# Four normalised columns in the value projection, offsets beside their values, and constants and weights of the second half made inside the first

## The reference, cut

```python
# x: (2, 128, 128, 128); _gn: GroupNorm over 32 groups of 4 channels, no weights
x = x + _L0_conv_ref(_gn(x), qkv_w, qkv_b, proj_w, proj_b, bias_table)
x = x + _L1_conv_ref(_gn(x), value_proj_w, value_proj_b, offset_mask_w, offset_mask_b,
                     output_proj_w, output_proj_b)

# _L0: 16 x 16 windows, 8 heads
attn = softmax(einsum('whnd,whmd->whnm', q, k) * scale + bias[None])
out = einsum('whnm,whmd->whnd', attn, v) @ proj_w.T + proj_b

# _L1: deformable convolution, G = 8 groups, K = 9 taps
v  = xt @ value_proj_w.T + value_proj_b            # values of each pixel
om = xt @ offset_mask_w.T + offset_mask_b          # 8 x 9 x (dx, dy, mask) of each pixel
loc_x = px + kx + off[..., 0]; loc_y = py + ky + off[..., 1]
# four corners of each (loc_x, loc_y), weighted bilinearly, times the mask, summed over the taps
out = einsum('nhwkgc,nhwkg->nhwgc', sampled, mask_t).reshape(N, L, C) @ output_proj_w.T + output_proj_b
```

## Time and profile before

| what | value |
|---|---|
| median of three runs | 3287.48 us (3285.68 to 3289.9) |
| the profiled execution | 3290.47 us |
| its span, first to last instruction | 3288.8 us |
| PE busy | 2733.5 us (83%), 22424 matmuls |
| PEld busy | 2192.2 us (67%) |
| DVE busy | 2719.8 us (83%) |
| ACT busy | 1828.7 us (56%) |
| POOL busy | 1162.0 us (35%) |

### The profile page before, as it was taken

The page is one execution under the profiler, slowest core; times in us unless marked ns, Lnnn a source line. Parts: engine busy times, 40 slices in busy tenths (PEclk is TensorE's granted clock), DMA queues, the critical chain, the costliest instruction groups (busy, mean ns, idle before and its releaser), DMA issues.

```text
span 3288.8 us, 77998 instructions
## 1 busy us (share of the span) xinstructions
PE 2733.5 (83%) x22424; PEld 2192.2 (67%) x22424; DVE 2719.8 (83%) x6553; ACT 1828.7 (56%) x3486; POOL 1162.0 (35%) x1557
## 2 busy tenths in 40 slices
PE   1888889999999999995677989998946799999986
PEld 0555555565565556564566888887835688888885
DVE  3888888888888888885667999999945799999996
ACT  0888888888888888884143443333202443334420
POOL 3333233333333333332446231346232441115550
PEclk9999999999999999998988999999978899999998
DMA  7889897888888898895553233333374433333334
GB/s 182 158 157 163 166 148 138 139 140 143 138 141 142 141 139 143 140 144 116 183 158 91 89 99 101 99 103 84 89 261 134 144 101 101 97 101 95 102 89 160
DMA packets 351779, 432.59 MB, mean 132 GB/s; under 512 B 42352, under 2 KB 275200, under 8 KB 346480
## 3 DMA queue, kind: packets, MB, share of 16 engines
q1 hardware_dynamic: 339696, 423.85, 58.5%
q0 software_dynamic: 11904, 6.44, 1.5%
HBM read 283.33 MB, written 147.09 MB: 131 GB/s over the span
## 4 chain that ended last, share of the span: by engine, by line
DVE 24%; issue 10%; DMA 6%; PE 5%; POOL 3%; DVEq 1%; ACT 1%; POOLq 1%; SPq 1%; ACTq 0%
DVE prod L1635 17%; DMA vring<-vals 3%; DVE tt L1619 2%; PE sum_ps L1429 2%; DVE my L1614 2%; DMA vring<-attended 1%; DVE x L1646 1%; PE sum_ps L1384 1%; ACT d_xn L1518 1%; DMA o_sel<-off_out,pos 1%; PE om_ps L1347 1%; POOL gath L1209 1%; PE sum_ps L1333 1%; POOLq L1216 1%; DMA out<-x 0%
## 5 line engine op out<-in xcount | busy, mean ns | idle before, releaser
L623 ACT ACTIVATE prob<-sbias,nmax 128x256 f32<-128x256 f32 x2048 | 903.9, 501 | 203.4 <-DVE nmax L716 201.0
L716 DVE CUSTOM_DVE_ANT_0 sbias<-s_ps,nbias 128x256 f32<-128x256 f32 x2048 | 768.0, 420 | 212.8 <-PE s_ps L508 201.4
L1635 DVE TENSOR_TENSOR prod<-vring,wt_ps 128x1920 f32<-128x1920 f32 (+3 forms) x512 | 898.8, 1815 | 18.8 <-DMA vring<-vals 11.9
L1384 PE MATMUL sum_ps<-d_ident,prod 128*128 128x128 f32 x6400 | 773.0, 279 | 83.5 <-DVE prod L1635 83.4
L1384 PEld LDWEIGHTS sum_ps<-d_ident,prod 128*128 128x128 f32 x6400 | 732.0, 144 | 131.8 <-DVE prod L1635 104.3
L521 PE MATMUL pt_ps<-a_ident,prob 128*128 128x128 f32 x4096 | 645.3, 280 | 140.5 <-ACT prob L623 137.5
L521 PEld LDWEIGHTS pt_ps<-a_ident,prob 128*128 128x128 f32 x4096 | 448.2, 141 | 284.3 <-DVE probT L725 134.3
L1484 ACT ACTIVATE hat<-off,one_col 128x576 f32<-128x576 f32 x128 | 140.7, 1099 | 700.6 <-DVE tt L1619 700.6
L508 PE MATMUL s_ps<-stack 96*128 96x256 bf16 x2048 | 396.6, 275 | 8.1 <-DMA stack<-parts_dram 7.4
L443 POOL CAST parts<-qk 128x1024 bf16<-128x1024 f32 x64 | 66.3, 1036 | 869.9 <-ACT qk L616 869.9
L725 DVE COPY probT<-pt_ps 128x512 f32<-128x512 f32 x512 | 351.9, 687 | 11.9 <-PE pt_ps L521 11.8
(11 more groups left out here) (170 smaller groups left out, 3382.2 us busy)
## 6 DMA issues: line engine op xcount, KB each, us to landing
stack<-parts_dram SPq DMA_DIRECT2D x768, 128.0 KB, 7.6
vring<-vals SPq DMA_DIRECT2D x270, 320.0 KB
parts_dram<-parts SPq DMA_DIRECT2D x64, 768.0 KB, 6.5
off_out<-off SPq DMA_DIRECT2D x64, 432.0 KB
strips<-x SPq DMA_DIRECT2D x68, 256.0 KB, 3.7
far_sums<-nothing SPq DMA_DIRECT2D x64, 256.0 KB, 2.1
attended<-on SPq DMA_DIRECT2D x256, 64.0 KB
x<-x SPq DMA_DIRECT2D x16, 1024.0 KB, 6.5
```

Source lines behind the costliest of these rows:

```text
L623: ins = nc.scalar.activation(prob[:, n % 4, half, :], sbias[:, n % SBIAS, half, :], ACT.Exp, bias=nmax[:, n % SBIAS, half:half + 1], scale ...
L716: ins = nc.vector.tensor_tensor_reduce(out=sbias[:, n % SBIAS, half, :], in0=s_ps[:, n % 2, half, :], in1=nbias[:, h, half, :], scale=1.0, ...
L1384: mm = nc.tensor.matmul(sum_ps[:, par, r * H:(r + 1) * H], prod[:, r % 2, dx, dy * C:(dy + 1) * C], ident[:], start=(r + dx + dy == 0), st ...
L1635: nc.vector.tensor_tensor(prod[:, r % 2, first:last].rearrange("p a (t c) -> p (a t) c", c=CG), vring[:, at:at + wide].rearrange("p a (t c ...
```

## The change

It has two parts.

**Constants and weights.** The tiles of weights, biases and constants are allocated ahead of both blocks, in a new class `Fixed`; the identity and the matrix of groups that `attention` makes are used by both. POOL writes the other constants at the start of `attention` (`fixed_tiles`) and splits the bias at its end (`fixed_bias`). SP loads the eight weights and writes the nine borders of `vals`, now from `nothing`, between the last two pairs of `attention`, and waits for the borders at that block's end. `deformable` loses its setup and eight of its 64 counted semaphores; `attention` has four more.

**Value projection.** Four buffers `xv`, laid into `prod[:, 0]`, take the place of the two `xn`. A normalise now waits for the values, and in the first steps the offsets, of four steps earlier. PE makes the offsets of a step right after its values. ACT copies them out one step later instead of two, and DVE searches them two steps later instead of three; all far-point searches of the first six steps now stand in steps 2 to 7, and the flags after step 5's addition.

```diff
+XVS = 4
 def attention(...):
...
             pair(PAIRS - 2, 0, left=1)
+            for t, src in late_weights:
+                sp.dma_start(t, src).then_inc(w_in, 16)
+            for col in (*range(PAD), *range(PAD + W, XP)):
+                sp.dma_start(at(vals, col * YP * C, [[NOTHING, YP * C // NOTHING], [1, NOTHING]]),
+                             nothing[0:YP * C // NOTHING, :]).then_inc(pad_out, 16)
+            for row in (0, PAD + H):
+                sp.dma_start(at(vals, (PAD * YP + row) * C, [[YP * C, W], [1, PAD * C]]),
+                             nothing[:, 0:PAD * C]).then_inc(pad_out, 16)
             pair(PAIRS - 1, 1, left=0)
...
             sp.wait_ge(far_cleared, count(16 * PAIRS))
+            sp.wait_ge(pad_out, count(16 * (XP - W + 2)))
...
             sample_info(nc, pool, info[:], info_int, info_step)
+            scratch = prob[:].rearrange("p n a k -> p (n a k)")[:, 0:KE].bitcast(I32)
+            fixed_tiles(nc, pool, fixed, scratch, consts)
...
+            fixed_bias(nc, pool, fixed, w_in, bias_split)
 def deformable(...):
...
+        xv = prod[:, 0].rearrange("p t c -> p (t c)")[:, 0:XVS * COLS * H].rearrange("p (s r y) -> p s r y", s=XVS, r=COLS)
...
                 def normalise(v):
-                    pool.wait_ge(v_done, count(b * GROUPS + v))
-                    pool.sem_inc(pool_passed, 1)
-                    if 2 <= v < AHEAD_OFF + 2:
-                        pool.wait_ge(om_done, count(b * GROUPS + v - 1))
+                    if v >= XVS:
+                        pool.wait_ge(v_done, count(b * GROUPS + v - XVS + 2))
                         pool.sem_inc(pool_passed, 1)
-                    nc.gpsimd.tensor_scalar(xn[:, 1], cols[:, v * COLS:(v + 1) * COLS, :], gn[:, 0:1], gn[:, 1:2],
+                        if v - XVS < AHEAD_OFF:
+                            pool.wait_ge(om_done, count(b * GROUPS + v - XVS + 1))
+                            pool.sem_inc(pool_passed, 1)
+                    nc.gpsimd.tensor_scalar(xv[:, v % XVS], cols[:, v * COLS:(v + 1) * COLS, :], gn[:, 0:1], gn[:, 1:2],
                                             ALU.mult, ALU.add).then_inc(vn_ready[1], 1)
...
         def _(pe):
-            pe.wait_ge(w_in, count(16 * 8))
-            pe.wait_ge(d_id, count(2))
-            pe.wait_ge(d_gm, count(3))
-            pe.wait_ge(ones_ready, count(4))
-            pe.wait_ge(bias_split, count(13))
...
-                        mm = nc.tensor.matmul(sum_ps[:, par, r * C:(r + 1) * C], xn[:, par, r, :], wvalue_sb[:],
+                        mm = nc.tensor.matmul(sum_ps[:, par, r * C:(r + 1) * C], xv[:, slot, r, :], wvalue_sb[:],
                                               start=True, stop=True)
                     mm.then_inc(v_done, 1)
                     if isinstance(v, int):
-                        if 0 <= v - 1 < AHEAD_OFF:
-                            offsets(v - 1, (v - 1) % 2)
+                        if v < AHEAD_OFF:
+                            offsets(v, xv[:, slot])
...
                     if slot % 2 == 0:
-                        act.wait_ge(v_done, count(b * GROUPS + v))
-                        if not isinstance(v, int):
-                            act.wait_ge(om_done, count(b * GROUPS + AHEAD_OFF))
-                        elif 2 <= v < AHEAD_OFF + 2:
-                            act.wait_ge(om_done, count(b * GROUPS + v - 1))
+                        if not isinstance(v, int) or v >= XVS:
+                            act.wait_ge(v_done, count(b * GROUPS + v - XVS + 2))
+                            if not isinstance(v, int):
+                                act.wait_ge(om_done, count(b * GROUPS + AHEAD_OFF))
+                            elif v - XVS < AHEAD_OFF:
+                                act.wait_ge(om_done, count(b * GROUPS + v - XVS + 1))
...
-                        nc.scalar.activation(xn[:, 0], src, ACT.Identity, bias=gn[:, 1:2],
+                        nc.scalar.activation(xv[:, slot], src, ACT.Identity, bias=gn[:, 1:2],
                                              scale=gn[:, 0:1]).then_inc(vn_ready[0], 1)
                     if isinstance(v, int):
-                        if 0 <= v - 2 < LEAD:
-                            read_offsets(first_spot(v - 2))
+                        if 0 <= v - 1 < LEAD:
+                            read_offsets(first_spot(v - 1))
...
-                    if isinstance(v, int) and 0 <= v - 3 < V_FIRST - 3:
-                        find_far(first_spot(v - 3))
-                    if isinstance(v, int) and 0 <= v - V_LAST < LEAD - (V_FIRST - 3):
-                        find_far(first_spot(v - V_LAST + V_FIRST - 3))
+                    if isinstance(v, int) and 0 <= v - 2 < LEAD:
+                        find_far(first_spot(v - 2))
...
-                        if v - 3 == EPOCH - 1:
-                            flags(first_spot(v - 3))
+                        if v - 2 == EPOCH - 1:
+                            flags(first_spot(v - 2))
```

More of the change, by code:

```diff
@@ new lines, in fixed_tiles @@
+def fixed_tiles(nc, pool, fixed, scratch, consts):
+    nc.gpsimd.memset(fixed.ones[:], 1.0).then_inc(consts, 1)
+    nc.gpsimd.memset(fixed.one_col[:, 0:1], 1.0).then_inc(consts, 1)
+    nc.gpsimd.memset(fixed.one_col[:, 1:2], -1.0).then_inc(consts, 1)
+    nc.gpsimd.memset(fixed.one_col[:, 2:3], 0.0).then_inc(consts, 1)
+    nc.gpsimd.memset(fixed.far_at[:].rearrange("p e i n -> p (e i n)"), 0).then_inc(consts, 1)
+    n_const = 5
+    one = [[1, 1]]
+    for dst, pattern, base, mult in (
+            (fixed.keytab[:], [[1, KE]], 1, 0),
+            (fixed.row_at[:], one, 0, KE),
+            (fixed.sum_at[:], [[EPOCH * COLS * H * G, B * EPOCHS]], 0, G),
+            (fixed.first_at[:, :, 0], [[EPOCH * COLS, EPOCHS]], 0, 0),
+            (fixed.first_at[:, :, 1], [[0, EPOCHS]], 0, 1)):
+        src = scratch[0:dst.shape[0], 0:dst.shape[1]]
+        nc.gpsimd.iota(src, pattern=pattern, base=base, channel_multiplier=mult).then_inc(consts, 1)
+        pool.wait_ge(consts, count(n_const + 1))
+        nc.gpsimd.tensor_copy(dst, src).then_inc(consts, 1)
+        pool.wait_ge(consts, count(n_const + 2))
+        n_const += 2
@@ L183, in attention @@
+def attention(nc, x, w_qkv, b_qkv, bv_row, rel_rev, attended, rel_rows, parts_dram, info_out, far_sums, vals, fixed, late_weights):
     with ExitStack() as ctx:
@@ L387, in pair, with at @@
                 store(p, 0, par)
+            def at(dram, offset, dims):
+                return bass.AP(dram.tensor, dram.offset + offset, dims)
             store_parts(0, 0)
@@ L780, in _, with deformable @@
             norm(2 * PAIRS - 1, 1, 1, (PAIRS - 1) // 2)
-def deformable(nc, x, attended, w_proj, bproj_row, w_value, bv_row, w_om, bom_row, w_out, b_out, vals, off_out, info_out, far_sums, out):
+def deformable(nc, x, attended, fixed, vals, off_out, info_out, far_sums, out):
     with ExitStack() as ctx:
@@ L1337, in _, with offsets @@
                 nc.tensor.matmul(a_ps[:, 0:2], gmat[:], ex[:], start=True, stop=True).then_inc(g_sum, 1)
-                def offsets(q, par):
+                def offsets(q, src):
                     n = b * GROUPS + q
@@ L1418, in group @@
                     if s.has(LEAD + 1):
-                        offsets(s.on(LEAD + 1).q, (s.place + LEAD + 1) % 2)
+                        offsets(s.on(LEAD + 1).q, xn[:, (s.place + LEAD + 1) % 2])
                     if s.has(LEAD) and (s.place + LEAD) % EPOCH == EPOCH - 1:
```

157 lines of the change are left out of this document (62 added, 95 removed).

## The result

The changed kernel takes 3249.49 us, the median of four runs (3247.57 to 3253.43), where the kernel before took 3286.84 beside it (four runs). The ratio is 0.9886, with a 95% interval from 0.9869 to 0.9904: 37.5 us less, between 31.6 and 43.1. The profiled execution took 3247.57 us, the lowest of the four; its span is 3245.9, 42.9 less than that of before. The forecast was 3247, with 40.3 us less.

A forecast was written before the change was run, and what follows sets the result against it. Engines waiting on each other in turn, in the setup between the halves and in the value projections, were taken as the bound. 11.5 - 0.24 plus both images' terms gave 40.3 us less: 3247 us, range 3236 to 3263.

The forecast's parts named there:

- the setup: Between the halves: SP's first load of x comes at 1534.75 instead of 1546.26, 11.5 us saved; 0.24 us lost earlier.
- steps 8 to 23: Value projection, sixteen columns: PE sets the pace at 1.04 us each instead of 1.376, gain 5.4 us an image.
- the end up to the first tap terms: Columns 24 to 31: first tap terms 6.3 us after column 24, gain 2.0 and 1.0 us in the two images.
- Start: Value projection's start: offsets of column 0 before values of column 1, gain 0.8 us an image, between 0 and 1.7.
- half of them take about twice as long, +1.0: Start term: the first offset matmuls begin at 1.2 GHz, costing 1.0 us against 1.74 saved.
- First steps: Columns 0 to 7: pitch 3.2 us a column, 21.5 us instead of 28.3, gain 6.8 us an image.
- the normalise and the values leave the circle: Columns 0 to 7: with four normalised columns only the single offset bank stays in the circle, 3.02 us a column.
- a little: Columns 0 to 7: allowance for ACT's normalise queued with its copy, taking the pitch from 3.02 to 3.2 us.
- The rival of the stores: Columns 8 to 23: row slots and DMA can't follow, pace stays 1.376 us, 2 x 5.4 lost, 3258; chance 0.09.
- Ports: Value projection: POOL's normalises and DVE block each other, six meetings of 1.2 us an image, 14.4 us, 3262; chance 0.08.
- Half of the first part: Columns 0 to 7: ACT's one queue keeps them at 4.0 us, half of 6.8 comes, 3254; chance 0.07.
- Tiles: Sampling: moved SBUF tiles slow the 512 products; 0.08 us each eats the gain, 0.15 gives 3324; chance 0.03.

The follow-up runs named there:

- the setup alone: Kernel before with only the constants and weights made in `attention`, the value projection as before: 3275.74 us, ratio 0.9974.
- The last kernel: Changed kernel with later second-group hats and first weights, first column loads one a step, 14 unread matmuls either side of PE's coefficient sum: 3228.59 us, ratio 0.9819.
- the kernel with two: Changed kernel with two normalised-column buffers instead of four, the new order of the offsets kept: 3265.04 us.
- the projection alone: Kernel before with only the four buffers and the new order of the value projection, the setup as before: 3261.38 us, ratio 0.9925.
- the kernel with 24 unread matmuls: Changed kernel with 24 matmuls that nobody reads on either side of PE's sum for the normalisation coefficients: 3250.28 us.

## Why the prediction was right, and where it was not

The time and the sign were right, and the sizes of most terms were: the setup (11.10 for 11.5), steps 8 to 23 (5.75 and 5.77 for 5.4, with PE as the bound, as forecast), the end up to the first tap terms (2.49 and 1.43 for 2.0 and 1.0; 1.23 and -0.37 behind them, for 0). Start and first steps together gave 6.66 and 8.60 for 7.6. The mechanism of the first steps was not the one that the prediction gave. Point by point:

- **Setup.** Its terms held, the 0.33 us push of the stores of `attended` included; the load came at 1535.18 for 1534.75, behind an issue of 0.41 us that the sum hadn't. That a microsecond saved there is one of the total is true only in the mean. In the pair of traces the coefficients of image 1 came 7.44 us earlier, not 11.1. The residual stage moves 16.8 MB, with the DMA engines at 0.75 and 0.80 of the time in the changed kernel; over the two images of all fourteen profiled executions it took 64.1 to 71.9 us, and one kernel had 65.71 in one image and 71.06 in the other. With the setup alone it took 66.93 and 67.45. Why it varies was not tried.
- **Start.** In this pair of traces the size failed, and the step that failed is the clock: "half of them take about twice as long, +1.0". In image 1 all of them did: 3.62 us where 1.83 is the full clock's. By the prediction's own ends (first normalise to ACT moving on) image 1 lost 0.53 us (6.73 before, 7.26 after), and image 2 gained 1.39 (7.56, 6.17), for 0.8. Over the profiled executions of all kernels with the old start and with the new one, without unread matmuls (4 and 16 passes), the means are 7.39 and 6.64, so 0.75 us are gained in the mean. The new start took 6.13 to 7.26 us: in image 2, at 6.17, only half of the offsets ran at the lower clock. Taking the offsets forward put them into the stretch where PE's granted clock is 0.50. The last kernel shows what that stretch costs: 2.76 us in image 1, 1.66 in image 2.
- **First steps.** The size was right. From ACT moving on at 1613.47 to the values of step 8 at 1634.57 it took 21.1 us, for 21.5 (its own terms add up to 21.3), and the copies of offsets stand 3.13 to 3.35 us apart, for 3.2. The step "the normalise and the values leave the circle", which leaves the offset bank alone in it at 3.02, failed. The circle that the trace shows is copy, size, normalise, values and offsets, 6.47 us for two steps; before, it was two normalises, one on ACT and one on POOL, each with its values and offsets, 8.92 us. What left it is POOL's normalise with its step on PE, which now run beside it. That the sum came out is in part luck: "a little" was added to 3.02 for ACT's one queue, and that queue is the pace. Nor were four columns needed for it: two buffers in the new order give the same circle, and so do four in the old.
- **Steps 8 to 23.** The buffers, and they alone, as the kernel with two shows. The rival of the stores was closer than the prediction made it: the DMA share is 0.94, not 0.61 x 1.376 / 1.02 = 0.82. The window holds two stores of offsets besides (432 KB each), whose packets are 0.13 of it; those of the value rows are 0.80. A packet of a value row took 28.9 ns in the mean, 27.1 before, and that did not come with the pace: it took 28.4 with the setup alone, at the pace of before, and 27.5 with the projection alone. Why it is longer with the new setup stays open. In the kernel with 24 unread matmuls late stores did hold up DVE, once an image.
- **Ports.** The rival's six meetings an image didn't come; one in each image did, in the first steps, and the chain doesn't go through it. Beside a normalise on POOL that starts at 1629.56, an instruction of DVE's flags took 1.07 us (1.08 in image 2), where its median is 0.226 and its longest in the kernel before was 0.229:

```profile
1629.75 1.07 DVE L1605 TENSOR_SCALAR far_at<-at,row_at 128x8 int32<-128x8 f32 x1
```

  With four buffers in the order of before two such instructions take 1.00 and 1.17 us beside POOL, and there they are on the chain, ahead of the search that ACT waits 3.08 us for. At the end, POOL's normalise behind the first tap terms, 3.49 us in the earlier trace rows, is gone: the last one is at 1656.31 and takes 1.23. What it meets is the product `my` (1.72 us here, 1.70 in the earlier trace rows, 1.05 in the median of all 64), before and after alike.
- **Half of the first part.** Its mechanism, one ACT queue for normalise and copy, is the one that the trace shows, but at 3.24 us a step and not 4.0, so the loss didn't come; the run with the offsets a step later on PE alone is this rival in a stronger form, where ACT's one queue made the first steps 14 to 16 us longer.
- **Tiles.** The products keep their time, 1813 ns for the 1815 of the earlier trace rows:

```profile
L1645 DVE TENSOR_TENSOR prod<-vring,wt_ps 128x1920 f32<-128x1920 f32 (+3 forms) x512 | 898.6, 1813 | 19.1 <-DMA vring<-vals 12.0
```

What was left out of the forecast is the noise of stages that the change doesn't touch: two residual stages and two samplings moved by 3.6, 5.5, 1.2 and 3.0 us between two executions. Single runs of the kernel before lay between 3278 and 3299 in one comparison, so a range of 27 us was not too wide.

## What to carry to other kernels

Where a producer and a consumer share few buffers, write down for each buffer what holds it to its end: in the steps with offsets bringing its last reader forward freed it as well as another buffer did, while the steps without them needed the buffers. Then look for the circle that is left: here a copy and a normalise in one queue, which neither edit took apart. An order moved on one engine has to be moved on the engines that read it, or an engine's own queue closes a new circle. Where a step is taken forward into a wait, price it at the clock that PE has there; a few matmuls that nobody reads, ended before the data come, gave that clock back.

## What the runs showed of the hardware

A POOL instruction on one column of numbers can take six times its usual time. In the far-point rounds of the changed kernel, this one takes 307 ns in the median of 40, and 1916 or 1917 ns three times (one line's instructions, min/median/max; then the timeline of POOL at the three places, and of DVE at the second):

```profile
L1266 POOL TENSOR_SCALAR sidx<-i_sel,sum_e x40: 305/307/1917, 1689.9 to 3147.8; 128x1 int32<-128x1 f32 x40
```

```profile
1936.05 1.92 POOL L1266 TENSOR_SCALAR sidx<-i_sel,sum_e 128x1 int32<-128x1 f32 x1 [0.28 <-POOL w L1262]
...
2567.32 3.00 DVE L1629 TENSOR_TENSOR tt<-hat,my 128x864 f32<-128x864 f32 x3
...
2567.51 1.92 POOL L1266 TENSOR_SCALAR sidx<-i_sel,sum_e 128x1 int32<-128x1 f32 x1 [0.28 <-POOL w L1262]
...
2959.83 1.92 POOL L1266 TENSOR_SCALAR sidx<-i_sel,sum_e 128x1 int32<-128x1 f32 x1 [0.28 <-POOL w L1262]
```

All three stand beside DVE's tap terms, which read two tiles in SBUF. Four more, of 560 to 730 ns, stand beside DVE's search for far points. Beside the products, which read one tile in SBUF and one in PSUM and fill most of the sampling, none is longer than 307 ns. That fits what the Trainium skill says ("SBUF — State Buffer", section "SBUF: two separate sides"): one pair of ports is held for a whole instruction by VectorE with two inputs in SBUF, or by GpSimd. The round at 2567.51 is on the chain. Whether such meetings are part of the 3.0 us by which the sampling of image 2 took longer than before is not shown: the kernel before had one there too (1917 ns), and why the stage was longer stays open.

A store of a value row landed 2.3 us after its issue when alone, and in the chains above 3.9 and 5.9 us when loads of columns were under way. Spreading the loads didn't shorten that, it moved it. The store of 4.05 us in the kernel with 24 unread matmuls stood behind a store of offsets and no load; after the change a store at the same place landed in 2.6 us, and why it was late there stays open.
